# Expert loop written out, with rings of 8 sorted-row, 8 base-row and 4 result buffers, in a one-core decoder layer

## The reference, cut to what matters

```python
x = hidden_states.reshape(-1, Dm)              # 1024 tokens of 256
logits = x @ router_w
expert_idx = jnp.argmax(logits, axis=-1)
score = jax.nn.sigmoid(jnp.max(logits, axis=-1))
xs = x * score[:, None]
for e in range(n_experts):                     # 8
    m = (expert_idx == e)[:, None]
    xe = jnp.where(m, xs, 0.0)
    h = jax.nn.silu(xe @ gate_w[e]) * (xe @ up_w[e])
    out = out + jnp.where(m, h @ down_w[e], 0.0)
shared = jax.nn.silu(x @ shared_gate_w) * (x @ shared_up_w) @ shared_down_w
return (out + shared).reshape(S, B, Dm)
```

## Time and profile before

| | us |
|---|---|
| median of 3 runs | 166.57 |
| lowest and highest | 164.66, 167.26 |
| span of the profiled execution, first to last instruction | 155.8 |
| total of the profiled execution | not given with the run |
| busy: TensorE (PE) | 119.9, 77% of the span |
| busy: VectorE (DVE) | 108.1, 69% |
| busy: ScalarE (ACT) | 69.8, 45% |
| busy: GpSimd (POOL) | 101.7, 65% |

### The profile page before, as it was taken

The page is one execution under the profiler, slowest core; times in us unless marked ns, Lnnn a source line. Parts: engine busy times, 40 slices in busy tenths (PEclk is TensorE's granted clock), DMA queues, the critical chain, the costliest instruction groups (busy, mean ns, idle before and its releaser), DMA issues. The chain is left out here.

```text
span 155.8 us, 2769 instructions
## 1 busy us (share of the span) xinstructions
PE 119.9 (77%) x709; PEld 97.2 (62%) x710; DVE 108.1 (69%) x303; ACT 69.8 (45%) x164; POOL 101.7 (65%) x145
## 2 busy tenths in 40 slices
PE   0199997997599658669879794459999979999700
PEld 0158986993387338347659594327878859888500
DVE  2672596949897999999699977122676866776510
ACT  3445878494396726794344401011434333343100
POOL 5346695696588828967858578605377776777540
PEclk9999999999999999975899999965999999999975
DMA  5997465236222251440222258283243334111000
GB/s 141 229 279 211 157 184 157 68 83 192 65 52 85 71 135 23 120 126 0 74 70 69 103 203 299 84 268 103 77 113 104 117 101 148 50 58 44 31 0 0
DMA packets 18206, 17.51 MB, mean 112 GB/s; under 512 B 4108, under 2 KB 17424, under 8 KB 18192
## 3 DMA queue, kind: packets, MB, share of 16 engines
q1 hardware_dynamic: 15792, 13.56, 30.8%
q0 software_dynamic: 1824, 3.22, 6.5%
q10 hardware_dynamic: 576, 0.56, 1.1%
HBM read 13.78 MB, written 5.38 MB: 123 GB/s over the span
## 5 line engine op out<-in xcount | busy, mean ns | idle before, releaser
L437 POOL TENSOR_TENSOR gu_lo<-stage,gu_hi 128x512 fp32r<-128x512 f32 x16 | 22.4, 1410 | 2.8 <-ACT gu_hi L502 2.8
L452 POOL DMA_INDIRECT tq<-base_rows,tid x15 | 15.4, 1026 | 13.1 <-DMA base_rows<-res 6.2
L457 POOL DMA_INDIRECT out_dram<-z,tid x15 | 15.2, 1012 | 7.6 <-DVE tid L851 2.6
L478 ACT ACTIVATE xn<-res,shift,rstd 128x256 f32<-128x256 f32 x22 | 12.0, 593 | 8.2 <-POOL shift L413 8.1
L405 POOL TENSOR_SCALAR vareps<-mv 128x2 f32<-128x2 f32 x16 | 4.2, 259 | 15.7 <-DVE mv L673 15.0
L409 POOL TENSOR_TENSOR rstd<-vareps,expo 128x2 f32<-128x2 f32 x16 | 12.4, 772 | 0.4
L1057 PE MATMUL bV<-shd,xn 128*128 128x256 f32 x32 | 9.6, 453 | 2.0 <-DVE xn L818 2.0
L670 DVE BATCH_NORM_STATS2 bn<-res 128x6 f32<-128x256 f32 x24 | 8.9, 413 | 3.0 <-DMA res<-in_x_dram 3.0
L437 POOL TENSOR_TENSOR dn_lo<-stage,dn_hi 128x512 fp32r<-128x512 f32 x8 | 11.0, 1371 | 0.0
L432 POOL DMA_INDIRECT x_sorted<-xs,dest x8 | 8.2, 1031 | 4.0 <-issue 2.6
L982 PE MATMUL bO<-wo,tq 128*128 128x256 f32 x32 | 7.8, 386 | 3.8 <-issue 2.8
(11 more groups left out here) (200 smaller groups left out, 386.4 us busy)
## 6 DMA issues: line engine op xcount, KB each, us to landing
stage<-in_L_ffn_gate_w_dram SPq DMA_DIRECT2D x8, 256.0 KB, 2.8
stage<-in_L_ffn_up_w_dram SPq DMA_DIRECT2D x8, 256.0 KB, 2.7
stage<-in_L_ffn_down_w_dram SPq DMA_DIRECT2D x8, 256.0 KB, 2.7
xs<-x_sorted SPq DMA_DIRECT2D x15, 136.0 KB, 2.2
res<-in_x_dram SPq DMA_DIRECT2D x4, 256.0 KB, 3.5
base_rows<-res SPq DMA_DIRECT2D x4, 256.0 KB
x_sorted<-pad SPq DMA_DIRECT2D x5, 136.0 KB, 3.4
x_sorted<-pad ACTq DMA_DIRECT2D x4, 136.0 KB, 3.3
```

What stands on the lines that cost most here:

```text
L437: g.tensor_tensor(units[n][2], stage[:, n % RING], f32(units[n][1]), ALU.subtract).then_inc(unit_lo, 1)
L452: g.indirect_dma_start(rb[:, s % TILE_RING, :], None, base_rows, bass.IndirectOffsetOnAxis(tid[:, s:s + 1], 0), bounds_check=N - 1, oob_is ...
L457: g.indirect_dma_start(out_rows, bass.IndirectOffsetOnAxis(tid[:, s:s + 1], 0), ry[:, s % 2, :], None, bounds_check=N - 1, oob_is_err=Fals ...
L478: last = a.activation(dst[:, i, :], res[:, b * TB + i, :], ACT.Identity, bias=shift[:, kind, b, i:i + 1], scale=rstd[:, kind, b, i:i + 1])
```

## The change

The program's edits, in words:

- The loops on SyncE, TensorE, ScalarE and VectorE are written out in full. Slots, semaphore values and DRAM offsets that came from the loop's register become constants, except for expert and row numbers.
- TensorE reads expert numbers twice: 8 values ahead of gate_up(0), and 7 in pass s = 6, between rows_turn(9) and gate_up(8).
- `xg` and `rb` have 8 slots (`rb` takes its upper four from `xT2`), `ry` has 4 (the upper two from `ez`). SyncE loads eight tiles ahead of the last two base stores.
- Token ids are copied 4 tiles at a time: `token_ids(0)` behind rows_lo(1), `token_ids(4)` behind rows_lo(2), `token_ids(8)` and `token_ids(12)` at the end of passes 4 and 8. `tid_made` counts these copies.
- GpSimd issues up to seven gathers ahead, and in its loop the write of tile s goes ahead of gather(s+7).
- Some semaphores of the routing steps are merged into one that counts further, with the same waits.

```diff
@@ -101,11 +101,9 @@
     SIM_SCALE = float(D) ** -0.5
 
     MEM_SCALE = 0.25 * (1.0 - DECAY)
-    PEEL = 3
-    LOOPS = (NS - 3 - PEEL) // 2
-    REST = PEEL + 2 * LOOPS
-    TILE_RING = 2 * KT
-    ROUNDS = (NS - 3 - PEEL) // TILE_RING
+    TILE_RING = NT
+    RESULT_RING = 2 * TB
+    AHEAD = TILE_RING - 1
     RING = 4
     PROJ = 3
 
@@ -213,8 +211,8 @@
         xgT_hi, xgT_lo = xT1_hi[:, :, :, 0:P], xT1_lo[:, :, :, 0:P]
         hT_hi, hT_lo = xT1_hi[:, :, :, P:2 * P], xT1_lo[:, :, :, P:2 * P]
         rh = tg
-        rb = tq[:, :, :, :].rearrange("p b k s -> p (b k) s")
-        ry = z
+        rb_lower = tq[:, :, :, :].rearrange("p b k s -> p (b k) s")
+        rb_upper = xT2[:, :, :, :].rearrange("p b k s -> p (b k) s")
 
         bT, bU, bG, bQ, bV, bO, bS, bM = [bank(n) for n in ("bT", "bU", "bG", "bQ", "bV", "bO", "bS", "bM")]
 
...
@@ -263,7 +262,7 @@
         gu_done, rth_made, rt_made, rh_made = sem("gu_done"), sem("rth_made"), sem("rt_made"), sem("rh_made")
         th_done, hT_hi_made, hT_lo_made = sem("th_done"), sem("hT_hi_made"), sem("hT_lo_made")
         down_done, y_made = sem("down_done"), sem("y_made")
-        written = [sem("written0"), sem("written1")]
+        written = [sem(f"written{r}") for r in range(RESULT_RING)]
 
 
         def rows(w):
@@ -285,6 +284,14 @@
 
         def kvT(b):
             return kvT_all[:, b, :]
+
+        def rb(s):
+            q = s % TILE_RING
+            return rb_lower[:, q, :] if q < 2 * KT else rb_upper[:, q - 2 * KT, :]
+
+        def ry(s):
+            r = s % RESULT_RING
+            return z[:, r, :] if r < TB else ez[:, r - TB, :]
 
         def pad_regions(queue, engine, first, last):
             _, count = nc.values_load_multi_w_load_instructions(
@@ -366,16 +373,10 @@
                 load_rows(q, row[q])
             for b in range(B - 2, B):
                 store_base(b)
-            with sp.Fori(0, NS // TILE_RING - 1) as i:
-                row = first_rows(i * TILE_RING + TILE_RING, TILE_RING)
-                for q in range(TILE_RING):
-                    sp.wait_ge(tx_done, i * TILE_RING + (q + 1))
-                    sp.wait_ge(tid_made, i * TILE_RING + (q + 1))
-                    load_rows(q, row[q])
-            row = first_rows(NS - NS % TILE_RING, NS % TILE_RING)
-            for q in range(NS % TILE_RING):
-                sp.wait_ge(tx_done, NS - NS % TILE_RING - TILE_RING + q + 1)
-                sp.wait_ge(tid_made, NS - NS % TILE_RING - TILE_RING + q + 1)
+            row = first_rows(TILE_RING, NS - TILE_RING)
+            for q in range(NS - TILE_RING):
+                sp.wait_ge(tx_done, q + 1)
+                sp.wait_ge(tid_made, 1 if q < TILE_RING // 2 else 2)
                 load_rows(q, row[q])
 
 
@@ -446,26 +447,26 @@
 
 
             def gather(s):
-                pool.wait_ge(tid_made, s + 1)
+                pool.wait_ge(tid_made, s // (TILE_RING // 2) + 1)
                 if s >= TILE_RING:
                     pool.wait_ge(y_made, s - TILE_RING + 1)
-                g.indirect_dma_start(rb[:, s % TILE_RING, :], None, base_rows, bass.IndirectOffsetOnAxis(tid[:, s:s + 1], 0),
+                g.indirect_dma_start(rb(s), None, base_rows, bass.IndirectOffsetOnAxis(tid[:, s:s + 1], 0),
                                      bounds_check=N - 1, oob_is_err=False).then_inc(rb_in[s % TILE_RING], 16)
 
             def write(s):
                 pool.wait_ge(y_made, s + 1)
-                g.indirect_dma_start(out_rows, bass.IndirectOffsetOnAxis(tid[:, s:s + 1], 0), ry[:, s % 2, :], None,
-                                     bounds_check=N - 1, oob_is_err=False).then_inc(written[s % 2], 16)
+                g.indirect_dma_start(out_rows, bass.IndirectOffsetOnAxis(tid[:, s:s + 1], 0), ry(s), None,
+                                     bounds_check=N - 1, oob_is_err=False).then_inc(written[s % RESULT_RING], 16)
 
             pool.wait_ge(base_out, 16 * B)
-            for s in range(TILE_RING - 1):
+            for s in range(AHEAD):
                 gather(s)
             for s in range(NS):
-                if s + TILE_RING - 1 < NS:
-                    gather(s + TILE_RING - 1)
                 write(s)
-            pool.wait_ge(written[0], 16 * ((NS + 1) // 2))
-            pool.wait_ge(written[1], 16 * (NS // 2))
+                if s + AHEAD < NS:
+                    gather(s + AHEAD)
+            for r in range(RESULT_RING):
+                pool.wait_ge(written[r], 16 * len(range(r, NS, RESULT_RING)))
 
 
         @block.scalar
@@ -634,21 +635,10 @@
             rows_hi(1, 1, False)
             tile_tanh(0, 0, False)
             rows_hi(2, 0, True)
-            for s in range(PEEL):
-                tile_tanh(s + 1, (s + 1) % 2, s + 1 >= 2)
+            for s in range(NS):
+                if s + 1 < NS:
+                    tile_tanh(s + 1, (s + 1) % 2, s >= 1)
                 hidden_hi(s, s % 2, s >= 2)
-                rows_hi(s + 3, (s + 1) % 2, True)
-            with act.Fori(0, LOOPS) as i:
-                for j in range(2):
-                    s = i * 2 + (PEEL + j)
-                    r = (PEEL + j) % 2
-                    tile_tanh(s + 1, 1 - r, True)
-                    hidden_hi(s, r, True)
-                    rows_hi(s + 3, 1 - r, True)
-            for s in range(REST, NS):
-                if s + 1 < NS:
-                    tile_tanh(s + 1, (s + 1) % 2, True)
-                hidden_hi(s, s % 2, True)
                 if s + 3 < NS:
                     rows_hi(s + 3, (s + 1) % 2, True)
 
...
@@ -845,49 +835,46 @@
                 dve.wait_ge(rt_made, s + 1)
                 v.tensor_tensor(rh[:, r, :], rh[:, r, :], psGU[r][:, D:2 * D], ALU.mult).then_inc(rh_made, 1)
 
-            def rows_lo(s, r, q):
+            def rows_lo(s, r):
                 dve.wait_ge(xg_hi_made, s + 1)
                 v.tensor_tensor(xgT_lo[:, r], psX[r][:, :, 0:P], f32(xgT_hi[:, r]), ALU.subtract).then_inc(xg_lo_made, 1)
-                v.tensor_copy(tid[:, bass.ds(s, 1)], xg[:, q, D:D + 1].bitcast(U32)).then_inc(tid_made, 1)
+
+            def token_ids(first):
+                tiles = range(first, min(first + TILE_RING // 2, NS))
+                for s in tiles:
+                    dve.wait_ge(xg_in[s % TILE_RING], 16 * (s // TILE_RING + 1))
+                q = first % TILE_RING
+                v.tensor_copy(tid[:, first:first + len(tiles)].unsqueeze(2),
+                              xg[:, q:q + len(tiles), D:D + 1].bitcast(U32)).then_inc(tid_made, 1)
 
             def hidden_lo(s, r):
                 dve.wait_ge(hT_hi_made, s + 1)
                 v.tensor_tensor(hT_lo[:, r], psH[r][:, :, 0:P], f32(hT_hi[:, r]), ALU.subtract).then_inc(hT_lo_made, 1)
 
-            def result(s, r, n, q, m):
-
+            def result(s, r):
                 dve.wait_ge(down_done, s + 1)
-                dve.wait_ge(rb_in[q], (m + 1) * 16)
-                dve.wait_ge(written[r], n * 16)
-                v.scalar_tensor_tensor(ry[:, r, :], psY[r][:, 0, :], 0.5, rb[:, q, :], ALU.mult, ALU.add).then_inc(y_made, 1)
-
-            rows_lo(0, 0, 0)
-            rows_lo(1, 1, 1)
+                dve.wait_ge(rb_in[s % TILE_RING], 16 * (s // TILE_RING + 1))
+                if s >= RESULT_RING:
+                    dve.wait_ge(written[s % RESULT_RING], 16 * (s // RESULT_RING))
+                v.scalar_tensor_tensor(ry(s), psY[r][:, 0, :], 0.5, rb(s), ALU.mult, ALU.add).then_inc(y_made, 1)
+
+            rows_lo(0, 0)
+            rows_lo(1, 1)
+            token_ids(0)
             hidden(0, 0)
-            rows_lo(2, 0, 2)
-            for s in range(PEEL):
-                hidden(s + 1, (s + 1) % 2)
-                hidden_lo(s, s % 2)
-                if s >= 1:
-                    result(s - 1, (s - 1) % 2, (s - 1) // 2, (s - 1) % TILE_RING, (s - 1) // TILE_RING)
-                rows_lo(s + 3, (s + 1) % 2, (s + 3) % TILE_RING)
-            with dve.Fori(0, ROUNDS) as i:
-                for j in range(TILE_RING):
-                    s = i * TILE_RING + (PEEL + j)
-                    r = (PEEL + j) % 2
-                    hidden(s + 1, 1 - r)
-                    hidden_lo(s, r)
-                    done = PEEL + j - 1
-                    result(s - 1, 1 - r, i * (TILE_RING // 2) + done // 2, done % TILE_RING, i + done // TILE_RING)
-                    rows_lo(s + 3, 1 - r, (PEEL + j + 3) % TILE_RING)
-            for s in range(PEEL + ROUNDS * TILE_RING, NS + 1):
+            rows_lo(2, 0)
+            token_ids(TILE_RING // 2)
+            for s in range(NS + 1):
                 if s + 1 < NS:
                     hidden(s + 1, (s + 1) % 2)
                 if s < NS:
                     hidden_lo(s, s % 2)
-                result(s - 1, (s - 1) % 2, (s - 1) // 2, (s - 1) % TILE_RING, (s - 1) // TILE_RING)
+                if s >= 1:
+                    result(s - 1, (s - 1) % 2)
                 if s + 3 < NS:
-                    rows_lo(s + 3, (s + 1) % 2, (s + 3) % TILE_RING)
```

(46 more changed lines are left out.)

29 lines of the change are left out of this document (15 added, 14 removed).

## The result

| | median us (range, runs) | ratio to before, 95% interval |
|---|---|---|
| before | 165.62 (163.75 to 167.26, 4) | |
| changed | 171.29 (169.12 to 171.81, 4) | 1.029 [1.017, 1.042] |

The change made the kernel slower by some 3%. 165.4 was forecast, with 163.4 to 167.8 as the range; the result is outside it. The profiled execution of the changed kernel took 170.78 us with a span of 169.1, so only 1.7 us lie outside the span, not the 10.8 that the prediction carried.

What follows compares the result with a forecast made beforehand. Bounds: TensorE's dense products to about 147.4 us, then a tail from the two-buffer result ring and late GpSimd. Span 155.8 - 1.06 (tail) - 0.09 (TensorE) = 154.65, plus 10.8 outside: 165.4 us, range 163.4 to 167.8.

Steps and rivals of the forecast that it cites:

- the 10.8 that the prediction carried: Time outside the profiled span, median 166.57 less span 155.8, taken as 10.8 us and unchanged by the diff.
- Token ids four at a time, gathers up to 7 ahead: GpSimd's expert loop: 30 issues back to back without waits for single ids, TensorE as cover; price 0.
- The base: Starting point of the sum: profiled span of 155.8 us plus 10.8 us outside it, from which gains were taken.
- Result ring: End of the expert loop: four result buffers end waits for writes; last write at 149.07, not 150.13, gaining 1.06 us.
- Sorted-row ring: SyncE's eight loads ahead of the last base stores: stores 2.1 us later, first gather at 108.2; cost 0, up to +1.
- Register reads: TensorE's expert numbers: eight values in 1.25 us at cost 0; seven in 1.87, stalling tile 8's product 1.17 us.
- rule of pieces: Register reads go by pieces of 4, 2 or 1 values, 0.62 us each on TensorE, so eight cost 1.25 us.
- Rival B: Register reads in large pieces: eight values 0.62 us, second read 1.25, new stall 0.55; time 164.2 us, chance 0.17.
- Rival A: Register read ahead of product 0 grows by value: +0.93 us, late clock rise +1.5; time 167.9 us, chance 0.13.
- Loops written out: TensorE's loop entries: 1.26 us of idle time gone, less a new stall of 1.17 at tile 8; net gain 0.09.
- Rival C: GpSimd stays the bound: base stores sharing DMA engines delay the first gather, tail does not shrink; 166.2 us, chance 0.15.

Runs made afterwards that it cites:

- kernel with early ids: The changed kernel with token ids of tiles 8 to 11 and 12 to 14 copied after passes 2 and 6, not 4 and 8: 164.97 us, ratio 0.982.
- second profile of the kernel before: The unchanged kernel before, run and profiled again: median 168.28 us, ratio 1.008, profiled span 164.1 us in an execution of 165.88.
- writes in sevens: Written-out loops without gathers, result ring of 8, the 15 writes issued in groups of seven: span 164.5 us, against 151.5 without gathers and ungrouped.

## Why the prediction was wrong, point by point

**The step that failed** is in "Token ids four at a time, gathers up to 7 ahead": "GpSimd no longer waits for single token ids", its 30 issues run back to back, and "the price here is 0, with TensorE as the cover". It failed twice. The issues don't run back to back: ids of tiles 8 to 11 are copied at the end of pass 4, but the gather of tile 8 stands in GpSimd's queue ahead of the write of tile 2. The prediction reckoned with the rate of issue and never laid gather 8 beside the pass that copies its ids. And TensorE is no cover. Shown: earlier ids or a later gather give back 4 to 7 us, where the price was put at 0; late updates come with runs of issues at 0.3 us, and on the whole the longer the run, the later. What links the two, read from the timelines and not tried by itself: a stand makes a backlog, the backlog a longer run (8 and 7 issues behind the two stands, 2 to 4 in the kernel with early ids), the long run later updates, these a later pass 8, and so the next stand.

**The base.** 155.8 + 10.8 was taken as an ordinary execution. It was an undisturbed span and a median of others. The forecast of 165.4 was thus a sum of two things that don't belong together, and its terms were small beside the 8 us that the profile lacked. In the total the two errors cancel (the first three executions of before have their median at 166.57 either way); what they hid is that ordinary executions have late updates, which the profile of the earlier trace rows has not. The three given times could not be split between launch and span; that 10.8 us outside it was a guess should have widened the range.

**Result ring, 1.06 gained.** The wait went as forecast: no result of the end waits for a write, and the last writes are 1.27 apart (161.95 and 163.22). Its worth alone was 0.6 us of 164.8, not resolved, and the last write started at 163.22 where 149.07 was forecast.

**Sorted-row ring, 0.** Right. Eight loads took 4.02 us, 0.50 each (0.54 forecast), and the first gather started at 107.31, against 108.2 forecast. It was 106.07 in the earlier trace rows, but 107.59 in the second profile of the kernel before, so the eight loads cost it nothing that can be seen.

**Register reads.** The size was off. Eight values took 0.79 us (1.25 forecast), seven 1.26 (1.87 forecast); TensorE's queue in the changed kernel:

```profile
L1071 PEldq TENSOR_LOAD <-te x2: 788/1026/1263, 101.9 to 130.3; - x2
```

```profile
104.66 0.72 PE L888 MATMUL bG<-gu_hi,xT_hi 128*128 x2 [0.79 <-DVE xT_lo L840]
...
131.34 0.38 PE L1067 MATMUL bS<-ident,xs 128*128 128x128 f32 x2
131.87 0.73 PE L888 MATMUL bG<-gu_hi,xT_hi 128*128 x2 [0.15 <-issue]
```

Product 0 waits for VectorE here, and starts at 104.66, as before (104.50 in the earlier trace rows, 105.10 behind five values in the second profile). Ahead of the product of tile 8 there is 0.15 us of idle time where 1.17 was forecast. Over all profiles eight values took 0.78 to 1.08 us on TensorE and 0.53 on SyncE, seven took 1.08 to 1.26 and 0.94 to 1.46. So seven take longer than eight, and the time does not go by value. But the rule of pieces on which the forecast rested does not hold either: three values took SyncE 0.68 us in the earlier trace rows and 0.30 in the second profile of the same kernel, no more than four. Rival B had the size of the stall (0.55 or less) and of the second read right. The 200 ns a register of the Trainium skill (Runtime: NRT & Kernel Launch, "Instruction fetch mechanics") do not agree with 0.79 us for eight. Rival A, the one on the slower side, did not happen.

**Loops written out, 0.09 gained.** This term was too small: by itself the edit has a ratio of 0.986, some 2.4 us. How much of it is the loop entries, and how much a better fit of the issues to the passes, was not tried apart.

**Rival C** had the nearest thought, that GpSimd stays a bound and only the wait moves, but by the base stores, and at 166.2.

## What to carry to other kernels

A queue that runs in order is as fast as its oldest unready entry: when prefetches are moved further ahead in it, each must be laid beside the step that makes its operand, for ready work queues behind. Count the longest run of GpSimd's back-to-back indirect DMAs in the profile, and see when the readers of TensorE's results start meanwhile; a faster or deeper burst is not free here. And check that a profile's span and the timed runs belong together (run the unchanged kernel again) before terms of a microsecond are summed on it.

## What the runs showed of the hardware that was not expected

- While GpSimd issued indirect DMAs 0.3 us after one another, TensorE's semaphore updates came late: by up to 2.4 us in runs of 4, 1.7 to 4.8 in runs of 6, 3.8 to 7.4 in runs of 7 to 9 while TensorE was at work. The last ones came 0.7 to 1.6 us after the run, in four of four together with the landing updates of its last transfer. At 1.5 us between issues, or at 1.0 with small memsets between them, the largest was 0.2. What it is that holds them is open, and so is why the first profile of the kernel before had none, with 23 issues from 114.50 to 145.63 and no gap over 0.7 us between them.
- The granted clock fell to 0.50 soon after each of the changed kernel's three holds, but not always: with writes in sevens it stayed 1.00 until 153 us, behind a hold of 5.2 us with TensorE idle from 138.9 to 140.5. Its mean over the loop does not show the holds: over 104 to 154 us it was 0.90 in the changed kernel, 0.91 in the first profile of before (no hold, but 0.50 until 109), 0.97 in the second (six late updates).
- One VectorE instruction on 15 values took 4.35 us in every profile but the first (0.32), whatever GpSimd issued later. The first is also the only one with gathers and writes back to back and no late update; whether the two have one cause was not tried.
